# Attention columns copied by ScalarE from PSUM straight into the neighbour matrices

## What is computed

```python
# layer 0, 4 passes: K = 8 neighbours by distance in ctx_4096
p = _lrelu(points)
g = _group_point(p, idx_t)
c = jnp.einsum('oi,bin->bon', w_center[i], p)
gn = jnp.einsum('oi,bikn->bokn', w_neighbor[i], g)
points = (c + gn.sum(axis=2)) / (K + 1.0) + shortcut
# layer 1: k = 30 neighbours, three channels of ctx_4096 as coordinates
rel = pts[bidx, idx] - pts[:, :, None, :]
...
feat = jnp.concatenate([sph, sph - jnp.mean(sph, axis=-1, keepdims=True)], axis=-1)
h = lrelu(_bn(feat @ W1.T, g1, b1))
h = lrelu(_bn(h @ W2.T, g2, b2))
h = lrelu(_bn(h @ W3.T, g3, b3))
att = jax.nn.softmax(h[..., 0], axis=-1)
xk = x.transpose(0, 2, 1)[bidx, idx]
agg = jnp.einsum('bnkc,bnk->bnc', xk, att)
return x + agg.transpose(0, 2, 1)
```

## Time and profile before

| | |
|---|---|
| median of 3 runs | 839.86 us (838.81 to 840.01) |
| profiled execution | 837.86 us |
| its span | 835.8 us |
| mean granted TensorE clock | 0.957 of full |
| TensorE matmul busy | 748.1 us (90%) |
| VectorE busy | 660.7 us (79%) |
| ScalarE busy | 286.0 us (34%) |
| GpSimd busy | 211.6 us (25%) |
| moved by DMA | 73.43 MB |

### The profile page before, as it was taken

One profiled execution on the slowest core, in us unless ns is written; L12 is line 12 of the kernel. 1 busy time (PEld: TensorE's weight loads), 2 busy tenths in 40 slices (PEclk: granted clock), 3 DMA queues, 4 the chain that ended last, 5 costly groups with the idle time before them and its releaser, 6 DMA issues.

```text
span 835.8 us, 13373 instructions
## 1 busy us (share of the span) xinstructions
PE 748.1 (90%) x5530; PEld 607.7 (73%) x5530; DVE 660.7 (79%) x1033; ACT 286.0 (34%) x415; POOL 211.6 (25%) x158
## 2 busy tenths in 40 slices
PE   5879899899999999999999977979989869696958
PEld 4678688667788878788788856858868757474746
DVE  5777999499899999999979999797777757484701
ACT  7335553412541212110014324424535534353400
POOL 3124856933203113013103716404600000000000
PEclk9999999899999999999999999999999979898979
DMA  9620002020002002545400000000004646374681
GB/s 358 149 102 1 0 1 102 1 102 0 1 13 90 2 2 73 187 158 174 149 26 1 1 0 1 1 0 1 0 14 140 202 147 229 141 226 165 225 278 51
DMA packets 32699, 73.43 MB, mean 88 GB/s; under 512 B 11392, under 2 KB 11392, under 8 KB 30336
## 3 DMA queue, kind: packets, MB, share of 16 engines
q1 hardware_dynamic: 32496, 70.49, 24.7%
q10 hardware_dynamic: 144, 2.10, 0.7%
HBM read 49.37 MB, written 23.20 MB: 87 GB/s over the span
## 4 chain that ended last, share of the span: by engine, by line
PE 59%; DVE 17%; DMA 10%; ACT 7%; POOL 3%; issue 3%; SPq 0%; ACTq 0%; POOLq 0%; DVEq 0%
PE bank L1434 25%; DMA att_d<-scratch 7%; PE bank L1458 5%; PE bank L1413 4%; PE bank L1415 4%; PE bank L1414 4%; DVE scratch L982 3%; ACT scratch L757 3%; DMA nbr<-att_d 3%; PE bank L1332 3%; PE bank L1333 2%; PE bank L1334 2%; PE bank L1568 2%; DVE pts_l L930 2%; PE bank L1569 2%
## 5 line engine op out<-in xcount | busy, mean ns | idle before, releaser
L1434 PE MATMUL bank<-nbr,pts_l 128*128 128x512 f32 x1024 | 242.7, 395 | 7.9 <-DVE pts_l L930 7.8
L1434 PEld LDWEIGHTS bank<-nbr,pts_l 128*128 128x128 f32 x1024 | 192.5, 190 | 49.4 <-DVE pts_l L930 9.6
L477 POOL TENSOR_TENSOR pts_h<-scratch,pts_h 128x512 fp32r<-128x512 f32 x58 | 85.9, 1486 | 165.6 <-ACT pts_h L672 165.6
L1413 PE MATMUL bank<-wT,pts_h 128*128 128x512 f32 x256 | 106.5, 416 | 14.4 <-DVE pts_l L930 10.3
L757 ACT COPY scratch<-bank 128x512 f32<-128x512 f32 x64 | 70.6, 1127 | 99.2 <-PE bank L1518 61.2
L1414 PE MATMUL bank<-wT,pts_h 128*128 128x512 f32 x256 | 103.1, 403 | 0.0
L1415 PE MATMUL bank<-wT,pts_h 128*128 128x512 f32 x256 | 102.8, 401 | 0.0
L1332 PE MATMUL bank<-pts_h 128*128 128x512 f32 (+2 forms) x192 | 71.9, 374 | 13.9 <-DVE pts_l L829 10.1
L679 ACT CAST pts_l<-bank 128x512 fp32r<-128x512 f32 x64 | 37.2, 586 | 135.6 <-PE bank L1415 135.4
L672 ACT CAST pts_h<-scratch 128x512 fp32r<-128x512 f32 x58 | 35.6, 615 | 130.9 <-DVE scratch L925 127.3
L1413 PEld LDWEIGHTS bank<-wT,pts_h 128*128 128x128 f32 x256 | 50.1, 196 | 29.3 <-DVE pts_l L930 13.4
(11 more groups left out here) (192 smaller groups left out, 1320.2 us busy)
## 6 DMA issues: line engine op xcount, KB each, us to landing
att_d<-scratch SPq DMA_DIRECT2D x64, 256.0 KB, 2.2
nbr<-att_d SPq DMA_DIRECT2D x16, 1024.0 KB, 5.5
more<-a_rows SPq DMA_DIRECT2D x17, 480.0 KB, 4.3
scratch<-a_rows SPq DMA_DIRECT2D x15, 480.0 KB, 4.3
X<-in_ctx SPq DMA_DIRECT2D x12, 512.0 KB, 6.5
out_dram<-X SPq DMA_DIRECT2D x16, 256.0 KB, 5.7
more<-in_ctx SPq DMA_DIRECT2D x4, 512.0 KB, 6.9
scratch<-in_fside_BxSxS SPq DMA_DIRECT2D x2, 1024.0 KB, 12.5
```

The costliest lines, as they stand in the source:

```text
L477: pool.tensor_tensor(p_l[:, t, hf * HALF:(hf + 1) * HALF], p32(n), p_h[:, t, hf * HALF:(hf + 1) * HALF].bitcast(F32), ALU.subtract).then_i ...
L1413: pe.matmul(bank[g % 3][:], p_h[:, t, cols], wT[:, 0, t, :], start=(t == 0), stop=False)
L1434: mm = pe.matmul(bank[3 + g % 3][:], y[:, m, t * P:(t + 1) * P], nbr[b][:, m, hf * HALF:(hf + 1) * HALF], start=(m == 0 and part_ == 0), s ...
```

## The change

- `spread_out` writes the bank straight into the neighbour matrix of its chunk, in consecutive elements, and reads PSUM with a step of 64 elements (8 reads of that step, then the next column). The staging tiles, the HBM tensor, the 64 stores, the 16 loads and their semaphores are gone.
- The first copy of a chunk waits until its neighbour matrix is free: chunk 0 for all of layer 0's aggregates on batch 0, chunk 1 for all on batch 1, chunks 2 and 3 for the attends of the chunk two earlier. Attend 4c waits for the sixteenth copy of its chunk.
- `onehots` makes two groups (16 columns) at once, in tiles of twice the size, which take the room of the staging tiles and more of the scratch; the first also waits until the last p is split.
- `NET` has one slot more: items 31 to 34, in two slots before, are in three. So T0 is 114, S0 is 120, and S_END is 16.

```diff
+        GP = 2 * GN
+        oa = [scratch[:, 512 + 1024 * i:1536 + 1024 * i].bitcast(BF16).rearrange("p (n a) -> p n a", n=GP)
+              for i in range(2)]
...
-               (24, 25), (26,), (27, 28), (29, 30), (31, 32), (33, 34), (35,), (), (37, 38), (39,), (40,), (41, 42),
+               (24, 25), (26,), (27, 28), (29, 30), (31,), (32, 33), (34,), (35,), (), (37, 38), (39,), (40,), (41, 42),
...
-            for q in range(CHUNKS * NG):
-                sp.wait_ge(s_scc, q + 1)
-                sp.dma_start(att_d[q // NG, :, (q % NG) * HALF:(q % NG + 1) * HALF],
-                             spread_s[q % 2]).then_inc(s_st[q % 2], 16)
-                for c, j in LOAD_AT.get(q, []):
-                    load_attention(c, j)
...
             def spread_out(q):
+                c = q // NG
                 act.wait_ge(s_sc, q + 1)
-                if q >= 2:
-                    act.wait_ge(s_st[q % 2], 16 * (q // 2))
-                act.copy(spread_s[q % 2].rearrange("p (x n) -> p n x", n=GN),
-                         bank[6 + q % 2][:].rearrange("p (n x) -> p n x", n=GN)).then_inc(s_scc, 1)
+                if q == 0:
+                    act.wait_ge(s_m, 2 * CT * (ITS - 1))
+                elif q == NG:
+                    act.wait_ge(s_m, 2 * CT * ITS)
+                elif q % NG == 0:
+                    act.wait_ge(s_f, CT * (c - 1))
+                act.copy(att_flat[c % 2][:, (q % NG) * HALF:(q % NG + 1) * HALF].rearrange("p (x n) -> p x n", n=GN),
+                         bank[6 + q % 2][:].rearrange("p (n x) -> p x n", n=GN)).then_inc(s_scc, 1)
...
-            def onehots(q):
-                n0 = (q // NG) * P + (q % NG) * GN
-                if q == 0:
+            def onehots(h):
+                n0 = GP * h
+                if h == 0:
                     dve.wait_ge(s_sct, 2)
                     dve.wait_ge(s_iota, 2)
                     dve.wait_ge(s_attq, CHUNKS)
-                if q >= 2:
-                    dve.wait_ge(s_sc, q - 1)
+                    dve.wait_ge(s_p1, 2 * CT * ITS)
+                if h >= 2:
+                    dve.wait_ge(s_sc, 2 * (h - 1))
...
                 if T0 + 3 <= g < T0 + 3 + CHUNKS:
                     att_parts(g - T0 - 3)
                 if g >= S0:
-                    onehots(2 * (g - S0))
+                    onehots(g - S0)
...
-                    onehots(q)
+                    if q % 2 == 0:
+                        onehots(q // 2)
...
                 if t == 0:
-                    pe.wait_ge(s_back[c], 16 * 4)
+                    pe.wait_ge(s_scc, NG * (c + 1))
```

More of the change, by code:

```diff
@@ L142, in build @@
             .rearrange("p (n i y) -> p n i y", i=4, y=2)
[L144 removed]
+        GP = 2 * GN
+        oa = [scratch[:, 512 + 1024 * i:1536 + 1024 * i].bitcast(BF16).rearrange("p (n a) -> p n a", n=GP)
               for i in range(2)]
[L146 removed]
+        mv = [scratch[:, 2560 + 1024 * i:3584 + 1024 * i].bitcast(BF16)
+              .rearrange("p (n i r) -> p n i r", n=GP, i=4) for i in range(2)]
+        eq = [scratch[:, 5280 + 256 * i:5536 + 256 * i].bitcast(BF16).rearrange("p (n r) -> p n r", n=GP)
               for i in range(2)]
[L148 to L149 removed]
         iota_a = scratch[:, 4992:5056].bitcast(BF16)
         iota_k = scratch[:, 5056:5072].bitcast(BF16)
[L153 removed]
         w_flat = wT[:].rearrange("p h t c -> p (h t c)")
@@ L234, in build @@
         s_attq = sem("att_parts_ready")
-        s_st = [sem(f"spread_stored{i}") for i in range(2)]
-        s_back = [sem(f"attention{c}_loaded") for c in range(CHUNKS)]
         s_oa = sem("a_onehot_ready")
@@ L278, in build @@
         TAIL = 4
-        QUARTER = NG // 4
-        FREE_AT = [max(1, 2 * (16 * (ITS - 1) - S0 + 1)), S_END + 1, S_END + 4 * TAIL + 2, S_END + 8 * TAIL + 1]
-        LOAD_AT = {}
-        for c in range(CHUNKS):
-            for j in range(4):
-                q = max(NG * c + QUARTER * (j + 1) + 1, FREE_AT[c] + 2 * j)
-                LOAD_AT.setdefault(min(q, CHUNKS * NG - 1), []).append((c, j))
         block = st.enter_context(nc.Block())
@@ L1517, in spread @@
                     for i in range(2):
-                        mm = pe.matmul(bank[6 + q % 2][:, n * 2 * KP:(n + 1) * 2 * KP], oa[q % 2][:, n],
-                                       mv[q % 2][:, n, 2 * i:2 * i + 2].rearrange("p h r -> p (h r)"),
+                        m = (q % 2) * GN + n
+                        mm = pe.matmul(bank[6 + q % 2][:, n * 2 * KP:(n + 1) * 2 * KP], oa[q // 2 % 2][:, m],
+                                       mv[q // 2 % 2][:, m, 2 * i:2 * i + 2].rearrange("p h r -> p (h r)"),
                                        start=(i == 0), stop=(i == 1))
```

41 lines of the change are left out of this document (11 added, 30 removed).

## The result

The changed kernel takes **795.71 us** (median of 4 runs, 795.49 to 796.65), the kernel before, in the same rounds, 839.93 us (838.81 to 840.68). The ratio is 0.948, 95% interval 0.946 to 0.949: 44.2 us or 5.3% less. The forecast was 794.0 us, with a range of 788 to 806.

What follows compares the result with a forecast made beforehand. Bound: the HBM round trip, then TensorE. First attend at 664.7 plus 121.5 of attends plus 0.3 of edges gives 786.5; plus 3.2 to the span's end, 2.06 over it and 2.0 to the median: 794.0 us, range 788 to 806.

Steps and rivals of the forecast that it cites:

- The round trip: Spread columns stored to HBM and loaded back: removing it ends 37.8 us of store waits and 30.6 us of load waits.
- TensorE is the next bound: Once the round trip is gone, TensorE's own pace sets the tail, 8.38 us for an attend with four spreads.
- The copy's price: ScalarE's copy with the stepped PSUM read takes 0.65 us instead of 1127 ns; chunk edges wait 0.3 us in all.
- The rival of a read that costs as much as the stepped write: ScalarE's copy stays at 1.13 us, costing 2.9 us more, 797 us (up to 802); chance 0.24.
- VectorE's pairs: One-hots for 16 columns take 2.86 us where two groups took 3.32; costed at nothing, TensorE barely covering it.
- VectorE hands the one-hots over late: Rival: one-hot pairs come one microsecond late in eight attends, plus some clock, 802 to 804 us; chance 0.13.
- The slots: An added network slot lets the seventh pass's first aggregate end 2.5 us earlier, near 568.8; first spread near 625.7 us.
- products that wait for y_low near 600 us: Sign of being wrong: in the network's slots, products waiting for the low part y_low.
- the exponential's cover: Exponential and index columns move from under an aggregate (3.7 us) to under a product (2.7 us); charged 0.9 us.
- the later slots lose: Rival: the exponential delays VectorE, TensorE waits for y_low, the clock falls; 3 to 6 us, 797 to 800; chance 0.08.
- The tail: All attends, 121.5 us: eight at 8.38 us, four without transposes at 7.94, four without spreads at 5.68.
- The sum: First attend near 664.7, last matmul 786.5, end of span 789.7, profiled run 791.8, median 794.0 us.

Runs made afterwards that it cites:

- e1: The kernel before with the direct copy only, one-hots and slots as before: 796.74 us, ratio 0.948.
- e4: The changed kernel with the copy in the other order, writing with a step and reading PSUM consecutively: 798.83 us, ratio 0.951.
- e9: The changed kernel with the x tiles turned one slot earlier, so no low part stands before the ninth pair of one-hots: 794.01 us, ratio 0.946.
- the square: Four kernels with the direct copy: one-hots single or in pairs, slots old or new; mark to end 243.7, 247.3 (old slots), 241.7, 243.6 us (new).
- e12: The changed kernel once more, unchanged, measured in a later run: 794.87 us, ratio 0.946.
- e8: The changed kernel, but each chunk's first attend waits for an added 512 KB load issued after the chunk's last copy: 819.64 us, ratio 0.977.
- e10: The changed kernel with e9's earlier turns, and the very first pair of one-hots made in two halves: 793.57 us, ratio 0.946.

## Why the prediction was right

**The round trip.** Right, and the whole gain: e1 alone gives 43.6 us. "TensorE is the next bound" holds: 70.0 of 70.0 us busy.

**The copy's price.** I took 0.65 us from the row of 661; it is 588 ns. My row was too high: the same kind of copy in the products took 586 ns in the kernel before as well (line 679). The rival of a read that costs as much as the stepped write was wrong in its price. What it would cost came out to the tenth, 2.9 us for e4's copies of 1.12 us, but in part by luck. Its first attend is 1.3 us later, where I had 1.4. Of the rest, I had 0.5 us more at each of three edges and it is 0.4; the wait of spread 16, which my sum did not have, is gone (1.42 us); and 1.9 us of slower matmuls, which it did not have either, make up for both. The Trainium skill ("SBUF — State Buffer", note in the section "Door 1: The DMA port swizzle") gives a penalty for each new line of SBUF; of PSUM's shorter lines it says that access that is not contiguous slows down matmuls. I had carried that over to ScalarE's read. For the write into SBUF the trace agrees, 1121 against 588 ns; for ScalarE's read of PSUM my carrying over fails, 588 ns with a step of 256 bytes against 586 without.

**VectorE's pairs.** The durations came out as worked out (0.42 and 1.22 us) and an attend in full swing shows no wait. But "I cost it at nothing" was wrong at the two starts: spreads 0 and 16 each wait for a pair that has nothing running ahead. At the first I had the wait (1.9 us; it is 2.05). At the second I had none. VectorE's timeline of the change shows it:

```profile
666.55 0.69 DVE L1178 TENSOR_TENSOR pts_h<-bank,pts_h 128x512 fp32r<-128x512 f32 x1 [0.94 <-ACT pts_h L741]
...
668.63 1.22 DVE L1170 TENSOR_TENSOR scratch<-scratch,more 128x2048 bf16<-128x2048 bf16 x1
```

```profile
669.95 0.63 PE L1496 MATMUL bank<-scratch 128*128 128x64 bf16 x16 [1.42 <-issue]
```

The last low part (line 1178) stands in VectorE's program before the ninth pair, waits 0.94 us for ScalarE's rounding, and the pair ends at 669.85. The view names no releaser for the wait (`issue`); that it is VectorE's, e9 shows, where it is gone. This is the rival "VectorE hands the one-hots over late" in a small form: once, not in eight attends.

**The slots.** Mechanism right for the low parts, size somewhat large; one of my signs of being wrong came. The rows that answer to the earlier trace rows, TensorE and VectorE:

```profile
555.74 0.50 PE L1390 MATMUL bank<-wT,pts_h 128*128 128x512 f32 x1 [1.78 <-DVE pts_l L909]
570.36 1.33 PE L1411 MATMUL bank<-nbr,pts_l 128*128 128x512 f32 x4 [1.39 <-DVE pts_l L909]
...
606.83 0.51 PE L1390 MATMUL bank<-wT,pts_h 128*128 128x512 f32 x1 [1.05 <-DVE pts_l L909]
```

```profile
569.62 1.28 DVE L909 TENSOR_TENSOR pts_l<-bank,pts_l 128x512 fp32r<-128x512 f32 x2
```

The waits of 0.28 and 1.85 us are gone and one of 1.39 has come. Behind the 1.85 us the products' matmuls took 0.63 us each in the kernel before, at the lower clock; behind the 1.39 us the clock is 1.00 (570 to 580 us). With the 2.42 us between the marks taken off, the last four matmuls of the aggregate end at 570.36 + 1.33 - 2.42 = 569.3 (forecast 568.8; before 571.3), so 2.0 us gained, not 2.5; and near 604.4 (606.83 - 2.42) a product waits 1.05 us for a low part. I had named products that wait for y_low near 600 us as a sign of being wrong, and charged 0.9 us for the exponential's cover. It is the start of what the rival "the later slots lose" describes. VectorE waits longer for the exponential, first before, then in the change, and the low part stands behind that:

```profile
597.72 0.65 DVE L1141 TENSOR_REDUCE small<-scratch 128x16 f32<-128x480 f32 x1 [2.59 <-ACT scratch L729]
```

```profile
604.26 0.65 DVE L1120 TENSOR_REDUCE small<-scratch 128x16 f32<-128x480 f32 x1 [4.11 <-ACT scratch L703]
```

The clock stays at 1.00 there (600 to 621 us), so it costs 1 us and not the rival's 3 to 6.

The first spread is at 629.21 - 2.42 = 626.8 (forecast 625.7), the first attend at 667.55 - 2.42 = 665.1 (forecast 664.7), its wait 0.72 us (1.4). So 0.7 of the 1.1 us by which the first spread was late came back by luck: the rounding copy and the two copies before the first attend start 0.5 us apart, where I had added up 0.66 and twice 0.65. As a whole the slots gain 2.0 to 3.7 us against the old ones by the square. I costed the new slots together with the pairs; that the two roughly cancel was not in the text.

**The tail.** VectorE's results, which mark the attends: the fourth and fifth, and the last two.

```profile
702.97 0.69 DVE L1224 TENSOR_TENSOR X<-bank,X 128x512 f32<-128x512 f32 x1 [0.78 <-PE bank L1548]
711.51 0.69 DVE L1224 TENSOR_TENSOR X<-bank,X 128x512 f32<-128x512 f32 x1 [0.78 <-PE bank L1548]
...
785.83 0.69 DVE L1224 TENSOR_TENSOR X<-bank,X 128x512 f32<-128x512 f32 x1 [4.99 <-PE bank L1548]
791.50 0.69 DVE L1224 TENSOR_TENSOR X<-bank,X 128x512 f32<-128x512 f32 x1 [4.99 <-PE bank L1548]
```

Within a chunk they are 8.39 us apart (forecast 8.38), across an edge 8.54 (0.15 for the edge; forecast 0.1), the last ones 5.67 (5.68). From the first attend to the last result it is 791.50 - 667.55 = 123.9 us, where I had 121.8: 1.4 us are the wait of spread 16, and 0.15 what the three edges took over my 0.3. The remaining 0.5 us is, in part at least, the time from a last matmul to its result; no row here separates it. From there to the end it is 3.1 us (3.2).

**The sum.** With the marks aligned the span is 794.6 - 2.4 = 792.2 us, forecast 789.7: 0.4 us before the first attend and 2.1 behind it. The largest single miss is the pair's wait at spread 16, at nothing in my sum. In the median 1.7 us were missed; that this is less than the 2.5 us of the aligned spans is scatter between executions (795.49 to 796.65, and 794.25 to 796.02 in e12), not merit.

## What to carry to other kernels

A round trip through HBM that only rearranges data can cost more than its waits: each edge's gap was paid once as idle time and once more in the clock behind it (2.2 us on 4.4 in e8). Before giving it up as the price of the layout, price the strided access side by side: on ScalarE the step belonged on the PSUM read. Larger instructions save fixed cost on an engine that is not the bound, and are paid at each start of a pipeline, where the first consumer waits for the whole of the first one: make the first one small, as e10 did.
